# Bringing the first rows of layer 2 to all partitions: a row in DRAM in place of products with ones

## What is computed

```python
lap_x = x[:, :, left] - 2.0 * x + x[:, :, right]      # reflected at the borders; lap_y along the tokens
y = zX * lap_x + zY * lap_y + zR * x * (1.0 - x)
lt = y[:, 1:17]                                        # 16 tokens
even, odd = lt[:, ::2], lt[:, 1::2]
m1 = (even[:, :4, :, None] * odd[:, :4, None, :]).reshape(B, 2048, 512)
m2 = (even[:, 4:, :, None] * odd[:, 4:, None, :]).reshape(B, 512, 2048)
h = gelu(y @ W1.T + scale * y @ m1.T + b1)
out = x + h @ W2.T + scale * h @ m2.T + b2
```

## Time and profile before

| what | value |
|---|---|
| time, median of 3 runs | 1335.46 us (1335.28 to 1336.07) |
| profiled execution | 1335.95 us, span 1334.7 us |
| TensorE busy | 1330.6 us, 100% of the span |
| VectorE, ScalarE, GpSimd busy | 78%, 60%, 19% |
| granted TensorE clock | 1.00 of full speed, all along |
| DMA | 253.52 MB, mean 190 GB/s |

### The profile page before, as it was taken

One profiled execution on the slowest core, in us unless ns is written; L12 is line 12 of the kernel. 1 busy time (PEld: TensorE's weight loads), 2 busy tenths in 40 slices (PEclk: granted clock), 3 DMA queues, 4 the chain that ended last, 5 costly groups with the idle time before them and its releaser, 6 DMA issues.

```text
span 1334.7 us, 17125 instructions
## 1 busy us (share of the span) xinstructions
PE 1330.6 (100%) x5901; PEld 1100.4 (82%) x5901; DVE 1035.7 (78%) x1775; ACT 794.3 (60%) x1376; POOL 256.1 (19%) x257
## 2 busy tenths in 40 slices
PE   9999999999999999999999999999999999999999
PEld 7888888888888888888888888888888888888887
DVE  8878799858897688976899768996689967665343
ACT  7654567645775566754577546675467754666432
POOL 1000122301232012320132201331022310232000
PEclk9999999999999999999999999999999999999999
DMA  8765377767778577875868667787767866667661
GB/s 245 195 155 151 81 204 213 203 213 204 180 212 196 189 213 198 203 197 197 208 188 223 183 215 196 193 218 180 224 179 205 214 181 207 161 187 167 176 190 55
DMA packets 140070, 253.52 MB, mean 190 GB/s; under 512 B 13648, under 2 KB 37456, under 8 KB 139984
## 3 DMA queue, kind: packets, MB, share of 16 engines
q1 hardware_dynamic: 121888, 201.03, 47.0%
q0 software_dynamic: 17520, 49.81, 22.5%
q10 hardware_dynamic: 576, 1.60, 0.3%
HBM read 189.34 MB, written 63.05 MB: 189 GB/s over the span
## 4 chain that ended last, share of the span: by engine, by line
PE 100%; DVE 0%; issue 0%; DVEq 0%
PE po L636 17%; PE po L638 17%; PE po L637 17%; PE ph L624 15%; PE ph L620 15%; PE ph L622 15%; PE ph L601 1%; PE ph L630 0%; PE po L580 0%; PE ph L663 0%; PE po L694 0%; DVE xr L1362 0%; PE po L594 0%; PE ph L594 0%; PE po L586 0%; PE po L588 0%
## 5 line engine op out<-in xcount | busy, mean ns | idle before, releaser
L636 PE MATMUL po<-W2h,gh 128*128 128x512 f32 x1020 | 396.8, 389 | 0.0
L637 PE MATMUL po<-W2l,gh 128*128 128x512 f32 x1020 | 396.8, 389 | 0.0
L638 PE MATMUL po<-W2h,gl 128*128 128x512 f32 x1020 | 396.8, 389 | 0.0
L624 PE MATMUL ph<-yh,W1l 128*128 128x512 f32 x896 | 348.6, 389 | 0.0
L622 PE MATMUL ph<-yl,W1h 128*128 128x512 f32 x896 | 348.6, 389 | 0.0
L620 PE MATMUL ph<-yh,W1h 128*128 128x512 f32 x896 | 348.6, 389 | 0.0
L638 PEld LDWEIGHTS po<-W2h,gl 128*128 128x128 f32 x1020 | 191.5, 188 | 39.8
L636 PEld LDWEIGHTS po<-W2h,gh 128*128 128x128 f32 x1020 | 191.5, 188 | 39.7
L637 PEld LDWEIGHTS po<-W2l,gh 128*128 128x128 f32 x1020 | 191.4, 188 | 39.7
L622 PEld LDWEIGHTS ph<-yl,W1h 128*128 128x128 f32 x896 | 168.2, 188 | 35.0
L620 PEld LDWEIGHTS ph<-yh,W1h 128*128 128x128 f32 x896 | 168.2, 188 | 34.9
(11 more groups left out here) (122 smaller groups left out, 1370.2 us busy)
## 6 DMA issues: line engine op xcount, KB each, us to landing
W2s<-in_w_dram SPq DMA_DIRECT2D x124, 256.0 KB, 3.9
R<-in_w_dram POOLq DMA_DIRECT2D x62, 512.0 KB, 7.3
uv_scratch<-UVs SPq DMA_DIRECT2D x112, 256.0 KB, 4.3
UVs<-uv_scratch SPq DMA_DIRECT2D x112, 256.0 KB, 3.9
X<-in_xT_dram SPq DMA_DIRECT2D x56, 390.0 KB, 4.8
xr<-in_x_dram SPq DMA_DIRECT2D x16, 1024.0 KB, 5.5
xr<-in_b_dram POOLq DMA_DIRECT2D x16, 1024.0 KB, 10.6
out_dram<-xr SPq DMA_DIRECT2D x64, 256.0 KB, 2.2
```

Of the source, the lines that this page charges most:

```text
L624: mm = e.matmul(bank[:, :], W1l[:, f, blk, wc], yh[:, q, c, :], start=False, stop=c == 1, skip_group_check=not first)
L636: e.matmul(po[t][:, :], gh[:, lt, st], W2h[:, k, :], start=i == 0 and lt == 0, stop=False)
L637: e.matmul(po[t][:, :], gh[:, lt, st], W2l[:, k, :], start=False, stop=False)
L638: return e.matmul(po[t][:, :], gl[:, lt, st], W2h[:, k, :], start=False, stop=i == NI - 1 and lt == 1)
```

## The change

The third row no longer goes by TensorE. ScalarE issues a DMA that stores 4 by 128 elements of `SA` (one element of 4 bytes at a time) to a new small tensor `row_scratch` in DRAM, once the six steps of `s_sc` are done. SyncE waits for that store (`d_row2`) and issues a load that broadcasts the 4 by 128 row to all partitions of `EB2` (`d_f0`). `fold(0, 0)` waits for `d_f0`. `diagonals(2)`, `even_row(2)`, the copy from `po[3]` and TensorE's wait on `s_rows2` go away. The load of x tile 4 moves from ScalarE's queue to SyncE's, ahead of tiles 5 to 7.

```diff
+    R2 = nc.dram_tensor("row_scratch", (4, 128), f32, kind="Internal").ap()
...
-            return ((s_rows2, 1), (d_f1, 16), (d_f2, 16), (d_e2, 16))[j]
+            return ((d_f0, 16), (d_f1, 16), (d_f2, 16), (d_e2, 16))[j]
...
         @block.sync
-            for n in (5, 6, 7):
+            for n in (4, 5, 6, 7):
                 load_x0(n)
+            e.wait_ge(d_row2, 16)
+            e.dma_start(EB2[:, :, :], bass.AP(R2.tensor, 0, [[0, 128], [128, 4], [1, 128]])).then_inc(d_f0, 16)
             keep_W1(2)
...
         @block.tensor
-                    bank = (ph[1] if c < 2 else po[2], ph[3], po[3])[j]
+                    bank = (ph[1] if c < 2 else po[2], ph[3])[j]
...
             pair0(0)
-            even_row(2)
             for n in range(1, 4):
                 pair0(n)
...
-                if ready is s_w2h:
-                    e.wait_ge(s_rows2, 1)
...
         @block.scalar
-                    v = SA[:, c, 2 * j:2 * j + 1] if j < 2 else SA[:, 0, 8 + 2 * c:9 + 2 * c]
+                    v = SA[:, c, 2 * j:2 * j + 1]
...
             load_x0(3)
-            load_x0(4)
             e.wait_ge(d_pk, 16)
...
             scaled(0, 0)
+
+            e.wait_ge(s_sc, 6)
+            e.dma_start(R2.rearrange("c p -> p c"), SA[:, 0, 8:16:2],
+                        allow_slow_non_contiguous=True).then_inc(d_row2, 16)
             scaled(0, 1)
...
             scaled(0, 3)
-            diagonals(2)
             outer(0, 2)
...
             part0_h(1)
-            e.wait_ge(s_row, 3)
-            e.activation(EB2[:, :, :].rearrange("p a q -> p (a q)"), po[3][:, :], ACT.Copy).then_inc(s_rows2, 1)
             part0_h(2)
```

More of the change, by code:

```diff
@@ L92, in adaln_ffn_kernel @@
         d_keep, d_back = sems("d_keep0 d_keep1"), sems("d_back0 d_back1")
-        s_rows2, d_f1, d_f2, d_raw0, d_raw1 = sems("s_rows2 d_f1 d_f2 d_raw0 d_raw1")
+        d_row2, d_f0, d_f1, d_f2, d_raw0, d_raw1 = sems("d_row2 d_f0 d_f1 d_f2 d_raw0 d_raw1")
         d_e1, d_e2, d_td, d_us, d_vs, d_xr, d_xa = sems("d_e1 d_e2 d_td d_us d_vs d_xr d_xa")
```

## The result

The changed kernel takes 1344.18 us (median of 6 runs, 1343.31 to 1345.51) beside 1335.74 for the kernel before in the same series: a ratio of 1.0063, 95% interval 1.005 to 1.0076. It is 8.4 us slower, where the forecast was 0.9 faster and the range ended at 1336.2.

What follows compares the result with a forecast made beforehand. TensorE was taken as the bound, busy 1330.6 of 1334.7 us. The terms, -0.89 + 0 + 0 + 0, took the median from 1335.46 to 1334.57 us; 8-in-10 range 1333.8 to 1336.2.

Steps and rivals of the forecast that it cites:

- Part 1: TensorE: even_row(2), 8 records at 14.42 us in the chain, goes away; -0.89 us.
- Parts 2 and 3: ScalarE: loses diagonals(2) (1.17 us) and the EB2 copy (0.62), gains one DMA issue (0.50); value 0.
- Part 5: Row through DRAM into EB2: full at 18.5 us, bound 27.0, fold needs it by 23.0; value 0, at worst 4.0.
- Part 6: SyncE's queue and shared DMA engines: W1 block 1 lands at 18.2 us, needed 18.3; value 0, at worst TensorE 4.2 late.
- Rival 2: VectorE's fold(0, 0): row late in EB2, each us past 23.9 costs one, up to 1338.6 us; chance 0.06.
- rival 3: Crowding of DMA: W1 block 1 lands at 22.9 us, +4.2 us, time 1338.8; chance 0.03.
- Part 4: Suppliers ScalarE and VectorE keep up with the earlier TensorE; W1h ready 19.35 for L630 at 19.78, 0.4 us spare.

Runs made afterwards that it cites:

- e2: Kernel before plus only the four-byte store, which nothing reads; EB2 still comes from TensorE: 1343.89 us, ratio 1.0057.
- e6: Changed kernel with 28 idle fp32 products on TensorE in front of the wait for W1 block 1: 1343.09 us, ratio 1.0055.
- e5: Changed kernel with W1 block 1 loaded plainly and early on SyncE's queue, its batch 0 outer product left out: 1343.77 us, ratio 1.0062.
- e8: Changed kernel storing four rows of 512 bytes (other values) instead of four-byte elements, same broadcast: 1335.87 us, ratio 0.9999.
- e9: Kernel before plus only the store, its 512 four-byte elements 64 bytes apart in DRAM: 1335.91 us, ratio 1.0.
- e13: Kernel before plus only the store, its 512 four-byte elements 16 bytes apart in DRAM: 1335.76 us, ratio 1.0001.
- e14: Kernel before plus only the store, cut to one row of 128 dense four-byte elements: 1343.05 us, ratio 1.0056.
- e12: Changed kernel, columns turned to rows by a TensorE product, stored as 4 x 512 bytes, broadcast issued after W1 block 1 landed: 1337.89 us, ratio 1.0016.
- e4: Changed kernel storing 16-byte pieces after a ScalarE copy, broadcast reading 2 KB pieces, fold reading with a stride: 1337.58 us, ratio 1.0018.
- e15: As e8, but the load into EB2 reads 256 KB of distinct addresses of W2, against the changed kernel: 1335.2 us, ratio 0.9998 to the kernel before.
- e11: As e8, but SyncE issues the broadcast only when W1 block 1 has landed: 1338.08 us, ratio 1.0016.
- e7: Kernel before plus only the store, 512 elements in the same 2 KB but each partition's four side by side: 1342.47 us, ratio 1.0048.
- e10: Kernel before plus only the store, cut to two rows, 256 dense four-byte elements: 1344.48 us, ratio 1.0064.

## Why the prediction was wrong

- Part 1 held: 0.89 us of TensorE are gone. Parts 2 and 3 held: the issue took 0.39 us, and the outer products started at 12.30.
- Part 5 failed, at the store. It was given 4.3 us, and at most 10.4 from the slowest row at hand; it took 15.0. The broadcast behind it took 7.5, inside its bounds of 6.6 and 10.4. EB2 was full at 28.4, where 18.5 was taken and 27.0 was the bound. The bounds came from transfers of another kind: none of them wrote neighbouring words one by one.
- Part 6 failed, and decided. It has the right victim, W1 block 1 on GpSimd's queue, needed at 18.3 and put at 18.2; it landed at 25.0. It counted only the broadcast against it ("because only the broadcast overlaps this load"), while the store's packets were there from about 10 to 21 us, and the store alone (e2) brings the block to 25 us. Its upper bound of 22.9 priced small packets at the queue's mean of 82 ns, and was not wide enough. The overlap was wrong too: it let the block share the engines with other traffic by bytes, but the block passes hardly a packet until SyncE's queue is running out, so what slows the x tiles delays it in full.
- The effect of a wait on the clock, 1.4 to 1.7 us here (e6, and the chain), was in no case's sum.
- The reading of the earlier trace rows that TensorE never waits from 1.13 us on was a little too strong: `raw0` took 4.19 us before for 3.44 us of records. That bears on the scatter between runs, not on the loss.
- Rival 2 (the row late at the fold) is real and of the same size, but lies behind rival 3 (e5). Rival 3 had the place, not the cause. Together they had 0.09.
- Part 4's reserve of 0.4 us at L633 was about right, and is why even the cheap store keeps nothing: in e8 the block took 8.0 us instead of 5.5, and PE waited 1.6.

The rule weighed in part 5, from the Trainium skill (DMA: Bandwidth & Descriptors, Specifications: below 512 B a read-modify-write), points the right way, but the trace bounds it: e9 makes 512 such writes at no cost. That a store on ScalarE's queue can cost another queue anything fits what the same page of the Trainium skill says in Issuing engines are not separate DMA queues: DMAs of SyncE, ScalarE and GpSimd run on the same 16 engines and interleave. Here the trace agrees on the shared engines, with 13.0 us against 5.5 for the GpSimd load, but hardly on the interleaving: GpSimd's queue passed 1 packet from 16 to 20 us while SyncE's passed 63.

Open: the unit of the neighbourhood. Density was changed by the same factor at 64 and at 512 bytes (e13), so the runs don't say which of them counts; nor do they show whether the 16 writes go one after another, as 0.69 us each would have it, and e14's short crawl speaks against that. Why GpSimd's queue passes next to nothing until SyncE's is running out is not shown either.

## What to carry to other kernels

A 2 KB transfer can cost more than a 512 KB one: look at how many separate small writes land next to each other in DRAM, not at the bytes. Turn a column to a row on chip before storing it (e12), store pieces of 16 bytes (e4), or put four-byte elements 16 bytes apart (e13). And a DMA's price is what it does to the transfer that is due next on any queue: ask which of those has less than a microsecond to spare.

## What was not expected of the hardware

- One row of 128 neighbouring four-byte stores is followed by DMA engines at some 36 GB/s (12 to 14 us in e14) and costs 7 us, nearly as much as 512 of them; 16 or 64 bytes apart, 512 are free (e13, e9).
- GpSimd's load passed no packet from 12 to 14 us in the kernel before and 1 from 16 to 20 us in the changed one, while SyncE's queue passed 294 and 63.
- 128 partitions that read the same 2 KB in 512-byte packets land at 16.9 us, though issued 1.2 us before a load from distinct addresses that lands at 15.8, and another queue's 512 KB takes 8.0 us instead of 5.9 (e8, e15).
- A wait of 1.0 to 1.6 us on TensorE left the granted clock at 1.00 (e4, e8, e11, e12); waits of 4.4 to 6.9 us were followed by work at a grant of 0.50, that is 1.2 GHz (e7, e2, e14, after, e10, e5).
